# A perceiver decoder on one core: one barrier between stages, the root's table, copies and key order of the second cross attention, and the place of the third one's output weights

## The reference

```python
for n in range(4):
    x = x + xattn[n](layernorm(x), ctx)   # [128, 256] over [12544, 256]
    x = x + attn[n](layernorm(x))
    x = x + ffn[n](layernorm(x))

def layernorm(x):
    return (x - mean(x)) / sqrt(var(x) + 1e-5)

def xattn1(x, ctx):                       # 16 heads of 16
    s = q @ k.T / 4 + bias                # bias [16, 128, 12544]
    return softmax(s) @ v @ Wo.T + bo

def xattn2(x, ctx):                       # 16 heads of 64, no bias
    return softmax(q @ k.T / 8) @ v @ Wo  # Wo [1024, 256]
```

## Time and profile before

| | us |
|---|---|
| median of 3 runs | 2990.39 (2987.64 to 2991.67) |
| profiled execution | 2986.41 |
| its span | 2984.7 |
| its mean granted clock of TensorE | 0.965 |
| PE busy / DVE / ACT / POOL | 2786.4 / 1769.0 / 1500.5 / 718.7 |
| l1x, from its first to its last norm-to-maximum row (start of l1x, end of its 16th maximum) | 963.5 to 1405.6 |

### The profile page before, as it was taken

How to read it: one execution, slowest core, us unless ns; L and a number is a source line. 1 busy time by engine, 2 the same in 40 slices (tenths; PEclk the granted TensorE clock), 3 DMA queues, 4 the chain that set the end, 5 groups by cost and what they waited for, 6 DMA issues and landing times. The chain is left out here.

```text
span 2984.7 us, 66864 instructions
## 1 busy us (share of the span) xinstructions
PE 2786.4 (93%) x24069; PEld 1862.3 (62%) x24069; DVE 1769.0 (59%) x3578; ACT 1500.5 (50%) x2407; POOL 718.7 (24%) x389
## 2 busy tenths in 40 slices
PE   7999999999898799999989999999999788999988
PEld 5555555555668466666556666666665685666678
DVE  3232323323143677887748888888888617888532
ACT  2333333333341488888336666666666333666521
POOL 2423232232000000000006666666666000000000
PEclk9999999999999799999999999999999698999989
DMA  6887877877725999997622222222222375655455
GB/s 210 290 268 255 252 255 256 252 256 240 251 98 183 405 390 390 390 392 279 225 101 67 66 67 65 66 66 64 67 64 66 99 233 128 169 158 155 120 210 182
DMA packets 331565, 578.28 MB, mean 194 GB/s; under 512 B 79792, under 2 KB 265976, under 8 KB 325752
## 3 DMA queue, kind: packets, MB, share of 16 engines
q1 hardware_dynamic: 331408, 576.06, 57.7%
HBM read 394.96 MB, written 181.04 MB: 193 GB/s over the span
## 5 line engine op out<-in xcount | busy, mean ns | idle before, releaser
L1762 POOL TENSOR_TENSOR l2x_sums<-l2x_sums,all_S 128x768 f32<-128x768 f32 (+1 forms) x195 | 474.6, 2434 | 189.4 <-ACT all_S L2086 183.6
L1966 DVE TENSOR_TENSOR all_S<-all_S,l2x_minus 128x1024 f32<-128x1024 f32 x224 | 381.9, 1705 | 1.9 <-ACT l2x_minus L2082 1.9
L1803 PE MATMUL l2x_key_bank<-ahead_ctx,early_nat_out 128*64 128x512 f32 (+1 forms) x1536 | 323.1, 541 | 0.0
L652 PE MATMUL prep_work<-prep_wv,prep_ctxT 128*128 128x512 f32 x688 | 300.3, 594 | 0.0
L1947 DVE TENSOR_TENSOR l2x_tops<-l2x_scores,l2x_tops 128x768 f32<-128x768 f32 (+1 forms) x208 | 223.4, 1074 | 117.6 <-PE l2x_scores L1819 117.6
L1399 ACT ACTIVATE l3x_pT<-l3x_turned 128x896 f32<-128x896 f32 x224 | 197.5, 916 | 145.4 <-PE l3x_turned L1249 140.5
L2086 ACT ACTIVATE all_S<-all_S 128x1024 f32<-128x1024 f32 x224 | 213.3, 952 | 96.9 <-DVE all_S L1966 96.9
L1148 ACT ACTIVATE all_S<-all_S,l1x_negmax 128x896 f32<-128x896 f32 x224 | 233.0, 1044 | 44.8 <-DVE l1x_negmax L1084 25.6
L991 PE MATMUL l1x_turned<-all_ident,all_S 128*128 128x128 f32 x1568 | 221.3, 282 | 21.7 <-ACT l1x_pT L1059 13.7
L1834 PE MATMUL l2x_out<-all_S,l2x_values 128*64 128x128 f32 x3136 | 226.3, 285 | 11.1 <-ACT all_S L2086 11.1
L2074 ACT COPY all_S<-l2x_scores 128x1024 f32<-128x1024 f32 x224 | 201.8, 901 | 65.4 <-PE l2x_out L1834 63.7
(11 more groups left out here) (685 smaller groups left out, 4694.1 us busy)
## 6 DMA issues: line engine op xcount, KB each, us to landing
l1x_bias<-in_fside_Bx16xSxS_dram SPq DMA_DIRECT2D x112, 896.0 KB, 7.2
scratch_k<-prep_kparts SPq DMA_DIRECT2D x84, 672.0 KB, 3.3
l1x_k_half<-scratch_k SPq DMA_DIRECT2D x32, 1568.0 KB, 9.8
l2x_values<-scratch_v SPq DMA_DIRECT2D x112, 256.0 KB, 2.6
scratch_k<-prep_kparts SPq DMA_DIRECT2D x56, 448.0 KB, 5.1
scratch_v<-prep_st_v SPq DMA_DIRECT2D x11, 2048.0 KB, 9.2
scratch_v<-prep_st_v SPq DMA_DIRECT2D x14, 1536.0 KB, 7.2
l2x_values<-scratch_v SPq DMA_DIRECT2D x112, 192.0 KB, 2.3
```

The costliest lines, as they stand in the source:

```text
L652: last = nc.tensor.matmul(w[:, h, :], ctxT[:, k, j * P:(j + 1) * P], wv2[:, k, h * 512:(h + 1) * 512], start=(k == 0), stop=(k == KT - 1))
L1762: nc.gpsimd.tensor_tensor(sums[odd][:, 0:n], sums[odd][:, 0:n], in_memory(u), ALU.add).then_inc(added, 1)
L1803: last = nc.tensor.matmul(keys_ps[u % 2][half * VW:(half + 1) * VW, 0:n], wk_cur[odd][:, k, :], ahead.piece[u // 2][:, k, c:c + n], start= ...
L1966: nc.vector.tensor_tensor(part, part, minus[:, :].unsqueeze(1).to_broadcast([P, blocks_of(u), P]), ALU.add).then_inc(shifted, 1)
```

## The change

1. A phase that is left no longer clears its semaphores and no longer has a barrier. The semaphores are collected in USED, and POOL clears them just ahead of the next block (`clear_used`, in every stage); a block still ends with its own barrier. One barrier is left at the very end.
2. At the end of ACT's stream in l0x, l0f, l1x, l1f, l2x, l2a, l2f, l3x and l3a a square root of a dummy (`com.root`) is added (`take_root`), ahead of which the table is then loaded; `com.root` is set by one more memset in init.
3. `by_vector` of l1x is (0, 2, 7, 11) instead of (3, 6, 9, 12).
4. In `load_first_head` the second half of head 1's keys and bias tile 3 come before the second half of head 0's values.
5. Wo of the third layer is loaded into `ahead.piece[0]`, the context's first piece, once all keys are made, among the value loads of the last head; for that SP's loop over the last pair of heads is written out. The turned result moves to the start of `com.S`.

```diff
@@ -60,8 +60,22 @@
         ph = Phase(nc, ctx, name)
         yield ph
-    nc.clear_and_free_semaphores(ph.sems)
-    nc.all_engine_barrier()
+    USED.extend(ph.sems)
+
+USED = []
+
+def clear_used(nc):
+    if USED:
+        nc.clear_and_free_semaphores(USED)
+        USED.clear()
+
+def take_root(nc, com):
+    nc.scalar.activation(com.root[:, :], com.root[:, :], ACT.Sqrt)
...
+        clear_used(nc)
         with nc.Block() as block:
...
@@ -929,10 +947,11 @@
         load_values(sp, 0, 0, True)
         load_bias(sp, 1, 1, False)
         load_bias(sp, 1, 2, False)
+        load_bias(sp, 1, 3, False)
+        load_keys(sp, 1, 1, False)
         load_values(sp, 0, 1, True)
-        for i in range(3, GRP // 2):
+        for i in range(4, GRP // 2):
             load_bias(sp, 1, i, False)
-        load_keys(sp, 1, 1, False)
...
             def _(act):
                 run.on_scalar(act)
+                take_root(nc, com)
...
-                              .rearrange("a p s -> (a p) s"), lag=5, by_vector=(3, 6, 9, 12), sum_ps=last_ps)
+                              .rearrange("a p s -> (a p) s"), lag=5, by_vector=(0, 2, 7, 11), sum_ps=last_ps)
...
-        wo, attT = scratch(8, D), scratch(8, P)
+        attT = scratch(8, P)
+        wo = ahead.piece[0][:, :, :].rearrange("p k n -> p (k n)")[:, 0:8 * D].rearrange("p (a b) -> p a b", a=8)
...
-                with sp.Fori(1, HEADS // 2) as i:
+                with sp.Fori(1, HEADS // 2 - 1) as i:
...
-                sp.wait_ge(weighed, HEADS * UNITS - 10)
-                sp.wait_ge(added, HEADS * UNITS - 10)
-                sp.dma_start(wo, a["L2_xattn_Wo"].rearrange("(k p) n -> p k n", p=P)).then_inc(wo_loaded, 16)
+                for odd in range(2):
+                    for u in range(UNITS):
+                        if odd and u == SLOTS:
+                            sp.wait_ge(keys_full, HEADS * UNITS)
+                            sp.dma_start(wo, a["L2_xattn_Wo"].rearrange("(k p) n -> p k n", p=P)).then_inc(wo_loaded, 16)
+                        load_values(HEADS - 2 + odd, odd, u)
...
+    clear_used(nc)
+    nc.all_engine_barrier()
```

More of the change, by code:

```diff
@@ L304, in _ @@
             def _(pool):
+                nc.gpsimd.memset(com.root[:, :], 1.0).then_inc(made, 1)
                 nc.gpsimd.memset(com.ident[:, :], 0.0).then_inc(made, 1)
                 nc.gpsimd.memset(com.identb[:, :], 0.0).then_inc(made, 1)
-                pool.wait_ge(made, 2)
+                pool.wait_ge(made, 3)
                 for m in (com.ident, com.identb):
@@ L310, in _ @@
                                             base=0, pattern=[[-1, P]], channel_multiplier=1).then_inc(made, 1)
-                pool.wait_ge(made, 4)
+                pool.wait_ge(made, 5)
 def high_parts(value):
@@ L820, in common @@
     com.ident, com.identb = sb("ident", [P, P]), sb("identb", [P, P], BF16)
+    com.root = sb("root", [P, 1])
     com.S, com.mx0 = sb("S", [P, SK]), sb("mx0", [P, GRP])
@@ L2417, in _ @@
                         activate(act, n_shared + g * EU * U + i, (n_shared + i) % 2, T, bias_col(g, j, u, act_at))
+                if name != "l3f":
+                    take_root(nc, com)
             def hidden(dve, n, r, t_n, bias_at):
```

## The result

The changed kernel took 2961.49 us in the median of 4 runs (2953.58 to 2962.34), against 2989.01 of the kernel before in 4 runs. The ratio is 0.9902, with a 95% interval of 0.9888 to 0.9915: 29.3 us less, 25 to 33 by the interval.

A forecast was written before the change was run, and what follows sets the result against it. PE, busy 93% of the span, was taken as the bound. Terms −10.8 − 0.6 − 3.5 − 5.0 − 4.0 = −23.9 took the profiled 2986.4 to 2962.5; the median, 4 us higher, gave 2966.5 us, range 2955 to 2976.

The forecast's parts named there:

- Barriers: Changes of stage: 20 phase exits at 0.55 us each, less 0.2 for clears; −10.8 us, from −12.5 to −3.3.
- The signs of being wrong: Wrong if l1x's steady head is outside 26.2 to 26.9 us, or DVE's stage-change gaps stay above 0.8.
- Root table: Norms 0.39 us shorter, counted in full at l2f, 0.2 for other stages together; −0.6 us, from −2.3 to +0.5.
- no gain: Start of l3x: the moved table load saves nothing, as DVE's scaling ends with POOL's memset, within 0.2 us.
- The bound of +0.5 for the clears: Start of l3x: worst case of the table's term, +0.5 us, if clears push the memsets and DVE's scaling back.
- Copies: Start of each l1x head: DVE copies slots 0 and 2; −0.25 us in 14 heads, −3.5, from −13 to +7.
- the walk: Start of an l1x head, chain followed by durations: turns 2 to 5 at 4.45, 5.65, 7.35 and 8.65 us.
- Rival B: l1x: copies pay in full, both waits go and nothing comes; −13 us instead of −3.5, 2957.0 in all; chance 0.06.
- C: l1x: DVE's copies hold the score banks longer; +7 us instead of −3.5, 2977.0 in all; chance 0.07.
- E: l1x: slower, both early copies lie fully in the score-bank chain; +30.5 us, 3000.5 in all; chance 0.02.
- Key order: First heads of l1x: 6.87 wait and 2.3 low clock go, 4.2 new waits come; −5.0 us, from −9.4 to −1.
- Wo: End of l2x: PE's 3.99 us wait for Wo goes; −4.0 us, from −5.0 to −1.6.

The follow-up runs named there:

- e2_root: Kernel before with only the dummy square root at the end of nine ACT streams and one more init memset: ratio 0.9994 (0.9984 to 1.0005), 1.8 us less.

## Why the prediction was right, term by term

The forecast was 2966.5 us with a range of 2955 to 2976; 2961.5 was measured. The five terms pay where they were put, and none of the rivals came true. Their sum was too small: 23.9 us, where the ratio says 29.3, 25 to 33. By ratios the five parts alone give 10.8 + 1.8 + 6.6 + 5.1 + 4.8 = 29.1 us, which fits the 29.3 of all together, but each of these is only good to 3 to 4 us, and their sum to about 7. By the stages in which they lie they give 11.0 and 0.8 (barriers), 1.7 (table), 4.2 (copies), 4.3 (keys) and 4.1 (Wo), 26.1 in all, which is within the interval; part of what is left may be l2a's (see the last section). What the terms missed is 1.1 of the table, 0.8 at l3x, and 0.7 to 1.1 of the copies. That the two profiled executions differ by 24.1, so close to the 23.9, is luck.

**Barriers** (−10.8): 11.0 by the gaps, 10.8 by the ratio. The slope between one, two and three exits was a sound price, and so was the 0.5 us left with no exit (0.53 measured). The signs of being wrong named a gap above 0.8, and one is there: l0f keeps 0.91 us, in every kernel with part 1. What is late there no run tells.

**Root table** (−0.6): at l2f 0.40 as put. The other stages, "about as late as the norm", were put at 0.2 together. This size was wrong: PE waited some 0.3 us for xn in four of them (l1x, l2a, l3a, l3f), and they give 1.3 (e2_root), so that the term is up to 1.7.

At l3x "no gain" from the table held: PE's turn of xn starts 3.03 us behind the stage's first row with barriers alone as in the changed kernel. But the reason, that DVE's scaling "should still end with the memsets", failed. Before, DVE was ready 0.07 us ahead of the first memset's end (2470.01, and 2468.28 + 1.80), and got in only behind the second. With the first memset pushed back by the clears it gets in between the two, and so it does with the table alone, where it is ready 0.4 us sooner. The bound of +0.5 for the clears had the wrong sign: they give 0.8. It is the exclusive pair of ports of the Trainium skill ("SBUF — State Buffer", "Who interferes with whom"): the trace agrees, as DVE's row ends within 0.2 us of the end of a memset each time, it took 0.61 with the table alone and 1.28 with the barriers alone (both ending with the first memset), and holding the memsets back gave 0.41. What I missed is that the pair is free between the two memsets, so that 0.4 us decides between waiting for one and for two.

As for the 1.38 us of drain behind a table load ("ScalarE: Activation LUTs", "What ACT_TABLE_LOAD costs", in the Trainium skill), in e2_root as in the changed kernel taking the load away shortened the reciprocal's wait by 0.39 and not by more.

**Copies** (−3.5): 0.33 us a head instead of 0.25, 4.6 us in 14 heads; the stage is 4.15 shorter. The mechanism was right, the size a third too small. ACT's first exponential of a head and PE's turn of slot 5 in the changed kernel:

```profile
1076.04 1.04 ACT L1167 ACTIVATE all_S<-all_S,l1x_negmax 128x896 f32<-128x896 f32 x1 [1.23 <-DVE l1x_total L1108]
...
1084.61 0.95 PE L1010 MATMUL l1x_turned<-all_ident,all_S 128*128 128x128 f32 x7
```

8.57 us lie between them; the walk had 8.65, and before it was 8.88. For turns 2 to 4 the rows give 4.30, 5.48 and 7.34, where the walk had 4.45, 5.65 and 7.35. One thing the walk doesn't explain: PE's listed waits in a head are no shorter, 0.54 + 0.39 + 0.54 = 1.47 us after and 0.19 + 0.47 + 0.46 + 0.24 = 1.36 before. By the windows of a steady head PE's busy time fell instead, from 25.31 to 25.00 us (1057.04 to 1083.84 before, 1075.46 to 1101.93 after), with the same instructions. The ends of matmuls are modelled, and waits too short to be listed would count as busy; that the gain lies in such waits is likely and not shown. Rival B (all waits go) is refuted by the listed waits, and C and E by the period.

**Key order** (−5.0): 4.3 alone. Both new waits are where they were foreseen, and in the changed kernel 2.95 + 1.22 = 4.17 us against 4.2. Alone, the key order bears out all three numbers of the sum: 7.3 for the old wait's 6.87, 2.35 for the low clock's 2.3, and 4.76 for the new waits' 4.2. The kernel with the key order alone and the changed one go on with the keys of head 2 at the same times (33.5 and 46.8 us behind the first maximum), so what PE gains ahead of them it waits for.

**Wo** (−4.0): 4.1 alone. The next bound was DVE's sum of blocks, as named. That the products "may stay as they are" was wrong by 1.4 us, as the clock rose sooner, and the 0.52 of the next wait and slower last products took most of it back: the term fits in part by luck.

## What to carry to other kernels

Read a barrier's price from the gaps where one, two and three of them stand in a row: the slope is the price, the rest is what stays. When a copy or a load is moved, walk the chain of the engine that takes it over; moving one more copy than pays costs nearly its whole duration in every turn of the loop. A long wait of PE costs the wait and the low clock behind it: the low clock behind the 6.87 us was worth 2.35, and where a wait went from 1.22 to 2.77 us the clock fell behind it. A change whose terms are each 0.1 to 0.4% is settled in the stage where each lies, since whole runs of this kernel differ by more than one term.

## What I had not expected of the hardware

The same instructions in a stage take different times with the granted clock, and which clock a stage gets differs between executions in which the work ahead is the same: the kernel with late memsets is the changed one up to l3x, and its l1f takes 17.4 us instead of 19.1. In l1f, the windows of 3 us from 3 us on, of before, of the changed kernel, and of the one with barriers alone:

```profile
1489.38:1492.38 3.00, 1.78 (x9) 1.43 (x10) 1.65 (x13) 1.35 (x4) 0.00 (x0) 0.83 1.02 386
...
1492.38:1495.38 3.00, 3.00 (x12) 2.44 (x11) 1.11 (x5) 0.58 (x1) 0.00 (x0) 0.60 1.04 423
```

```profile
1474.95:1477.95 3.00, 1.79 (x11) 1.44 (x11) 1.64 (x13) 1.35 (x4) 0.00 (x0) 0.92 1.00 350
...
1477.95:1480.95 3.00, 3.00 (x11) 2.33 (x10) 1.12 (x5) 0.58 (x1) 0.00 (x0) 0.51 1.03 421
```

```profile
1483.10:1486.10 3.00, 1.79 (x12) 1.40 (x13) 1.67 (x13) 1.35 (x4) 0.00 (x0) 1.00 1.00 350
...
1486.10:1489.10 3.00, 3.00 (x21) 2.69 (x20) 1.78 (x7) 1.17 (x2) 0.00 (x0) 1.00 1.04 420
```

The columns are length, busy time of PE, PEld, DVE, ACT and POOL, clock, DMA share and GB/s. PE is busy 1.78 or 1.79 us in the first window of all three. In before and in the changed kernel the clock then goes to its lower level, 1.2 GHz, for about 3 us; with barriers alone it stays at the upper one, 2.4 GHz, and the stage takes 17.4 instead of 20.1 and 19.1 us (1.1 of the 20.1 is the longer gap ahead of l2x). Seven profiles (the changed kernel and the six made from it) have the same code outside l1x and the start of l3x. In them l0a takes 81.5 to 84.8 us, l1f 17.4 or 19.1, l2x 842.4 to 846.5, l2a 32.8 to 34.4 and l3a 31.6 to 34.9. l2a is another case: in the seven without all five parts (before and its six) it takes 35.3 to 36.9 us, so that the two groups don't meet. The gap ahead of l2f is 0.6 of it and the table 0.35; some 1.6 us more, on the average, stay. Less those two, the shortest of the others (35.27) would be 34.3 and the groups just touch, so this is likely an effect of the parts together, and no run with one part shows it. In the window from 4 to 8 us of l2a the clock is 0.68 to 1.00 in the first seven and 0.50 to 0.67 in the others; why it is higher no run tells. l3x takes 359.5 to 366.2 us in those five of the seven that leave it as it is, and 358.2 to 365.7 in the kernels made from the one before; part of it is PE's waits for keys, 3.5 us in before and 8.5 in the changed kernel. So the 4.8 us by which l3x is longer in the changed kernel's profile are no effect of the change that a run supports. Both kernels gain or lose several microseconds by such turns of the clock and of DMA in any one execution, which is why the two profiled ones agree with the sum better than they had to.
